# Two layers of attention and feed-forward on one core: V products issued by pairs of steps, and PSUM's working banks in two pairs

## The reference, cut to what matters

```python
x = x + _L0_xattn_ref(_layernorm(x, axis=-1), ctx_1024, L0_xattn_Wq, L0_xattn_Wk, L0_xattn_Wv, L0_xattn_Wo)
...
q = (x @ Wq).reshape(B, S, H, D).transpose(0, 2, 1, 3)
k = (c @ Wk).reshape(B, N, D, H).transpose(0, 3, 2, 1)
v = (c @ Wv).reshape(B, N, D, H).transpose(0, 3, 1, 2)
mask = jnp.all(c == 0, axis=-1)[:, None, None, :]
scores = jnp.einsum('bhsd,bhdn->bhsn', q, k) * scale
scores = jnp.where(mask, -jnp.inf, scores)
att = jax.nn.softmax(scores, axis=-1)
out = jnp.einsum('bhsn,bhnd->bhsd', att, v)
out = out.transpose(0, 2, 1, 3).reshape(B, S, H * D)
return out @ Wo
```

## Time and profile before

| | |
|---|---|
| Median of 3 runs | 2168.86 us (2168.70 to 2173.09) |
| Span of the profiled execution | 2168.4 us |
| Mean granted clock of TensorE | 0.969 of full |
| PE busy (share of the span) | 2030.2 us (94%) |
| DVE busy | 1710.2 us (79%) |
| ACT busy | 1073.8 us (50%) |
| POOL busy | 1163.8 us (54%) |
| Stages 0 to 15 of the first attention | 85 to 1616 us |
| Steady stages | 96.2 and 99.0 us in turn, 2.1 more at a turn of the loop |

### The profile page before, as it was taken

The page is one execution under the profiler, slowest core; times in us unless marked ns, Lnnn a source line. Parts: engine busy times, 40 slices in busy tenths (PEclk is TensorE's granted clock), DMA queues, the critical chain, the costliest instruction groups (busy, mean ns, idle before and its releaser), DMA issues. The chain is left out here.

```text
span 2168.4 us, 35171 instructions
## 1 busy us (share of the span) xinstructions
PE 2030.2 (94%) x10757; PEld 1431.6 (66%) x10757; DVE 1710.2 (79%) x4048; ACT 1073.8 (50%) x1493; POOL 1163.8 (54%) x624
## 2 busy tenths in 40 slices
PE   5999999999999999999999999999986899859995
PEld 4666666666666666666666666666654688647774
DVE  7788878878887888888888878878756777767764
ACT  3445445453535455454535445454533699744442
POOL 0275755657475756656575656557674354314340
PEclk9899999999999999999999999999996999979997
DMA  3000000000000000000000000000000121022210
GB/s 94 1 1 16 1 3 4 14 1 4 18 1 1 4 16 1 3 18 1 1 4 16 1 4 1 1 1 1 1 0 21 60 88 58 25 76 62 61 46 23
DMA packets 54855, 40.84 MB, mean 19 GB/s; under 512 B 2500, under 2 KB 51596, under 8 KB 53644
## 3 DMA queue, kind: packets, MB, share of 16 engines
q1 hardware_dynamic: 54668, 38.57, 6.0%
HBM read 37.45 MB, written 1.11 MB: 18 GB/s over the span
## 5 line engine op out<-in xcount | busy, mean ns | idle before, releaser
L374 POOL TENSOR_TENSOR a_den<-a_den,a_probs 128x1024 f32<-128x1024 f32 x352 | 846.7, 2408 | 362.8 <-ACT a_probs L571 362.7
L571 ACT ACTIVATE a_probs<-a_probs,a_mask_col 128x1024 f32<-128x1024 f32 x416 | 478.9, 1151 | 578.6 <-DVE a_probs L740 578.5
L740 DVE TENSOR_TENSOR a_probs<-a_scores,a_shift 128x512 f32<-128x512 f32 x832 | 566.8, 686 | 180.1 <-PE a_scores L399 162.3
L681 DVE CUSTOM_DVE_ANT_0 a_work<-a_work,a_mask_row 128x400 f32<-128x400 f32 (+1 forms) x1024 | 572.7, 587 | 35.6 <-PE a_work L431 33.2
L479 PE MATMUL a_pv<-a_probs,a_V 128*64 128x256 f32 x3328 | 451.0, 392 | 5.8 <-ACT a_outT L578 3.8
L431 PE MATMUL a_work<-a_cT_hi,a_Q_hi 128*128 128x400 f32 (+1 forms) x1024 | 357.5, 380 | 2.6
L397 PE MATMUL a_scores<-a_Q_hi,a_cT_hi 128*128 128x512 f32 x832 | 340.5, 409 | 0.1
L398 PE MATMUL a_scores<-a_Q_lo,a_cT_hi 128*128 128x512 f32 x832 | 327.9, 394 | 0.0
L399 PE MATMUL a_scores<-a_Q_hi,a_cT_lo 128*128 128x512 f32 x832 | 326.5, 392 | 0.0
L479 PEld LDWEIGHTS a_pv<-a_probs,a_V 128*64 128x64 f32 x3328 | 202.5, 136 | 186.0 <-issue 116.3
L431 PEld LDWEIGHTS a_work<-a_cT_hi,a_Q_hi 128*128 128x128 f32 x1024 | 194.9, 190 | 137.1 <-issue 89.6
(11 more groups left out here) (319 smaller groups left out, 2855.9 us busy)
## 6 DMA issues: line engine op xcount, KB each, us to landing
m_gate_rows<-gate_scratch SPq DMA_DIRECT2D x8, 1024.0 KB, 4.7
a_c_nat<-in_ctx_dram SPq DMA_DIRECT2D x8, 768.0 KB
b_c_in<-in_ctx_dram SPq DMA_DIRECT2D x8, 768.0 KB
b_c_nat<-in_ctx_dram SPq DMA_DIRECT2D x8, 768.0 KB
m_w_raw<-in_L_ffn_W_dram SPq DMA_DIRECT2D x16, 256.0 KB, 5.0
a_acc<-in_x_dram SPq DMA_DIRECT2D x8, 128.0 KB, 2.0
out_dram<-tokens SPq DMA_DIRECT2D x4, 256.0 KB, 2.3
a_V<-in_L_xattn_Wq_dram SPq DMA_DIRECT2D x1, 512.0 KB, 6.8
```

Source lines behind the costliest of these rows:

```text
L374: nc.gpsimd.tensor_tensor(half, so_far, probs[:, buffer(c, j), :], ALU.add).then_inc(den_added, 1)
L571: nc.scalar.activation(probs[:, buffer(c, j), :], probs[:, buffer(c, j), :], ACT.Exp, bias=mask_col[:, c // 2 % 2, j // 2:j // 2 + 1]).the ...
L681: nc.vector.tensor_tensor_reduce(out=X[:, bank, :w], in0=X[:, bank, :w], in1=mask_row[:, off:off + w], scale=1.0, scalar=-3e38, op0=ALU.ad ...
L740: nc.vector.tensor_tensor(probs[:, buffer(c, j), pair * 2 * S:(pair + 1) * 2 * S], Sc[:, pair, :], shift[:, first:first + 2 * S], ALU.add) ...
```

## The change

It has two parts, in the first attention alone.

1. The products with V of an even step are no longer issued in that step, but in slot 1 of the odd step after it, right before the odd step's own. An even step has none.
2. The four banks of `X` become two pairs of banks, with one semaphore pair each. An item is twice as wide and there are half as many: eight and five transposed chunks instead of four at a time, Q of four heads, V of two chunks, maxima of 804 columns (two matmuls of 402, one custom instruction on DVE, one accumulator read), a spread of 1,024 columns, one item for all eight denominators, in slot 5. An item waits until the item two before has been taken out. `V_AFTER`, `LATE_V` and `SPREAD` get new slots, so that the items keep about their places: 43 instead of 85 of them in the first 92 slots where a context is prepared, 39 instead of 77 elsewhere. The chunks hold 13 x 128 = 1,664 columns, of which the maxima now use 1,608.

The sums of all products are as before. The diff, cut to its core:

```diff
@@ -112,18 +112,19 @@
     STEPS = 2 * NC
     SLOTS = 4 * STEPS
     STAGES = 2 * B
-    PIECES = [(0, 402), (402, 400), (802, 400), (1202, 400)]
+    PIECE = 402
+    HALF = 2 * PIECE
     UNITS = G8 * 2
 
-    BANKS = 4
-    TAIL = 3
-
-    V_AFTER = [1, 4, 6, 8, 10, 12, 14, 26, 38]
-    LATE_V = [95, 97, 100, 102]
+    PAIRS = 2
+    TAIL = 2
+
+    V_AFTER = [0, 2, 4, 6, 12]
+    LATE_V = [95, 100]
     MAX_END = 92
     SHIFTS = [83, 93]
     DIAG = [84, 88]
-    SPREAD = [92, 93, 98, 99]
+    SPREAD = [92, 98]
...
-            early += [("cT", i) for i in range(3)] + [("cxT", 3)] + [("mask", i) for i in range(4)]
-        early += [("q", i) for i in range(4)]
-        vs = [("v", c) for c in range(NC)]
-        for u in range(UNITS * 4):
+            early += [("cT", 0), ("cxT", 1)] + [("mask", i) for i in range(2)]
+        early += [("q", i) for i in range(2)]
+        vs = [("v", c) for c in range(0, NC, 2)]
+        for u in range(UNITS * 2):
             early.append(("max", u))
             if u in V_AFTER:
                 early.append(vs.pop(0))
...
-            slots[3].append(("den", 0))
-            slots[7].append(("den", 1))
+            slots[5].append(("den", 0))
...
-        X = es.enter_context(nc.psum_tensor("a_work", [P, BANKS, 512], F32))
+        X = es.enter_context(nc.psum_tensor("a_work", [P, PAIRS, 2, 512], F32))
...
-                            filled(pool, it, use_of(the_plan(it, c), "den", j - 2))
+                            filled(pool, it, use_of(the_plan(it, c), "den", 0))
...
-                    for ch in range(4 * i, min(4 * i + 4, NC)):
-                        last = nc.tensor.transpose(out[:, ch % 4 * P:(ch % 4 + 1) * P], c_nat[:, ch, :], ident[:, :])
+                    for ch in range(8 * i, min(8 * i + 8, NC)):
+                        last = nc.tensor.transpose(out[:, ch % 8 * P:(ch % 8 + 1) * P], c_nat[:, ch, :], ident[:, :])
                     if kind == "cxT":
                         pe.wait_ge(xn_ready, at(it, 2, s // 2 + 1))
                         for j in range(2):
-                            last = nc.tensor.transpose(out[:, (j + 1) * P:(j + 2) * P], xn_b[:, j, :], ident[:, :])
+                            last = nc.tensor.transpose(out[:, (j + 5) * P:(j + 6) * P], xn_b[:, j, :], ident[:, :])
                 elif kind == "mask":
-                    pe.wait_ge(flag_done, at(it, 8, s // 2 * 4 + i + 1))
-                    off, w = PIECES[i]
-                    last = nc.tensor.matmul(out[:, :w], ones_b[:, :], c_flag[:, off:off + w], start=True, stop=True)
+                    pe.wait_ge(flag_done, at(it, 4, s // 2 * 2 + i + 1))
+                    for k in range(2):
+                        off = (2 * i + k) * PIECE
+                        last = nc.tensor.matmul(X[:, bank, k, :PIECE], ones_b[:, :], c_flag[:, off:off + PIECE],
+                                                start=True, stop=True)
                 elif kind == "q":
-                    for k in range(2):
-                        h = s % 2 * G8 + 2 * i + k
+                    for k in range(4):
+                        h = s % 2 * G8 + 4 * i + k
                         last = split_product(out[:, k * S:(k + 1) * S], [g[:, h, :] for g in G], xnT,
                                              slice(0, D), slice(0, S))
                 elif kind == "v":
-                    last = split_product(out, cT[s // 2 % 2], Wv, slice(i * P, (i + 1) * P),
-                                         slice(s % 2 * G8 * HD, (s % 2 + 1) * G8 * HD))
+                    for k in range(min(2, NC - i)):
+                        last = split_product(X[:, bank, k, :], cT[s // 2 % 2], Wv, slice((i + k) * P, (i + k + 1) * P),
+                                             slice(s % 2 * G8 * HD, (s % 2 + 1) * G8 * HD))
                 elif kind == "max":
-                    off, w = PIECES[i % 4]
-                    last = nc.tensor.matmul(out[:, :w], Q[s % 2][0][:, i // 4 * P:(i // 4 + 1) * P],
-                                            cT[s // 2 % 2][0][:, off:off + w], start=True, stop=True)
+                    for k in range(2):
+                        off = (i % 2 * 2 + k) * PIECE
+                        last = nc.tensor.matmul(X[:, bank, k, :PIECE], Q[s % 2][0][:, i // 2 * P:(i // 2 + 1) * P],
+                                                cT[s // 2 % 2][0][:, off:off + PIECE], start=True, stop=True)
                 elif kind == "spread":
-                    if i < 2:
-                        pe.wait_ge(diag_done, at(it, 32, 8 * s + 4 * (i + 1)))
-                    else:
-                        pe.wait_ge(shift_steps, at(it, 20, 5 * s + 5))
-                    last = nc.tensor.matmul(out, ones_r[:, :], shift_diag[:, i % 2 * 4:i % 2 * 4 + 4, :], start=True, stop=True)
+                    for k in range(2):
+                        if i == 0:
+                            pe.wait_ge(diag_done, at(it, 32, 8 * s + 4 * (k + 1)))
+                        elif k == 0:
+                            pe.wait_ge(shift_steps, at(it, 20, 5 * s + 5))
+                        last = nc.tensor.matmul(X[:, bank, k, :], ones_r[:, :], shift_diag[:, 4 * k:4 * k + 4, :],
+                                                start=True, stop=True)
                 elif kind == "den":
 
-                    pe.wait_ge(den_added, at(it, 4 * (STEPS - 2), c * (STEPS - 2) - 1 + i))
-                    for k in range(2):
+                    for k in range(4):
+                        if k % 2 == 0:
+                            pe.wait_ge(den_added, at(it, 4 * (STEPS - 2), c * (STEPS - 2) - 1 + k // 2))
                         for odd in range(2):
-                            h = 4 * i + 2 * k + odd
+                            h = 2 * k + odd
                             last = nc.tensor.matmul(out[HD * odd:HD * odd + HD, k * S:(k + 1) * S], ones[:, :],
                                                     den[:, h * S:(h + 1) * S], start=True, stop=True)
...
-                        if part == 1:
-
-                            pv(it, c, j, 0)
-                            pv(it, c, j, 1)
+                        if part == 1 and j % 2 == 1:
+
+                            for both in (j - 1, j):
+                                pv(it, c, both, 0)
+                                pv(it, c, both, 1)
                         elif part > 1 and j + 2 < STEPS:
...
-                    nc.scalar.activation(V[:, s % 2, i, :], X[:, bank, :], ACT.Copy).then_inc(bank_free[bank], 1)
+                    n = min(2, NC - i)
+                    nc.scalar.activation(V[:, s % 2, i:i + n, :], X[:, bank, 0:n, :], ACT.Copy)\
+                      .then_inc(bank_free[bank], 1)
                 elif kind == "spread":
                     if c >= 0:
 
-                        act.wait_ge(shifted, shifts_of(it, c, STEPS - 2 + i // 2, i % 2 + 1))
-                    nc.scalar.activation(shift[:, i * 512:(i + 1) * 512], X[:, bank, :], ACT.Copy)\
+                        act.wait_ge(shifted, shifts_of(it, c, STEPS - 2 + i, 2))
+                    nc.scalar.activation(shift[:, i * 1024:(i + 1) * 1024], psum, ACT.Copy)\
                       .then_inc(bank_free[bank], 1)
                 elif kind == "den":
-                    nc.scalar.activation(rden[:, i * 512:(i + 1) * 512], X[:, bank, :], ACT.Copy)\
-                      .then_inc(bank_free[bank], 1)
+                    nc.scalar.activation(rden[:, :], psum, ACT.Copy).then_inc(bank_free[bank], 1)
...
-                    off, w = PIECES[i % 4]
                     filled(dve, it, use)
                     dve.nop(nofuse=True)
-                    nc.vector.tensor_tensor_reduce(out=X[:, bank, :w], in0=X[:, bank, :w],
-                                                   in1=mask_row[:, off:off + w], scale=1.0, scalar=-3e38,
+                    masks = mask_row[:, i % 2 * HALF:(i % 2 + 1) * HALF].rearrange("p (h n) -> p h n", h=2)
+                    nc.vector.tensor_tensor_reduce(out=X[:, bank, :, :PIECE], in0=X[:, bank, :, :PIECE],
+                                                   in1=masks, scale=1.0, scalar=-3e38,
                                                    op0=ALU.add, op1=ALU.max, accum_out=maxes[:, s % 2, i:i + 1])\
                       .then_inc(bank_free[bank], 1)
                 elif kind == "shift":
                     half = UNITS // 2
                     units = slice(i * half, (i + 1) * half)
...
-                        for quarter in (2 * j, 2 * j + 1):
-                            taken(dve, it, prep_use(it, c - 1, "spread", quarter))
+                        taken(dve, it, prep_use(it, c - 1, "spread", j))
```

More of the change, by code:

```diff
@@ L149, in prep_slots @@
             slots[DIAG[i]].append(("diag", i))
-        for i in range(4):
+        for i in range(2):
             slots[SPREAD[i]].append(("spread", i))
@@ L248, in attention_0 @@
         xn_all, wv_ready = sem("xn_all"), sem("wv_ready")
-        bank_full = [sem(f"bank{i}_full") for i in range(BANKS)]
```

(12 more changed lines are left out.)

74 lines of the change are left out of this document (36 added, 38 removed).

## The result

The changed kernel takes 2189.7 us (median; 2188.3 to 2191.9), 1.0084 of the kernel before, 95% interval [1.0070, 1.0097]: **slower by 0.84%** (the kernel before ran in 2170.9 us beside it), where 2162 was forecast. Its profiled execution spans 2188.9 us, 20.5 more than before. By the traces of the two, 11.0 of these lie in the opening stage (the first score product starts at 91.76 instead of 80.80), 8.5 between it and the last addition to the tokens (1560.96 instead of 1552.45), and 1 in the rest of the program.

The account below looks back on a forecast made before the run. PE sets the time in the first attention, with DVE close behind. Mode changes saved -78, waits +73, opening -2.5, a denominator copy +1: -6.5 us, from 2168.86 to 2162 us; this case 2148 to 2177, overall range 2110 to 2200.

Parts of the forecast that it names:

- The detour: PE's mode change between 64- and 128-column matmuls in the first attention: 0.35 us each, fifteen saved a stage, -78 us.
- 2x + y: PE, V and denominator products back to back: two groups of eight V matmuls (x) plus one mode change (y), 2.08 us.
- The pair of maxima: DVE, one maximum over two banks: 0.95 us start to start, 1.06 if nothing of two instructions is saved.
- rival (c): DVE, steps 9 to 22: pair of maxima costs 1.06 us, +32, 2194 us; chance 0.26 including unsaved mode changes.
- The waits for single late operands: PE waits: context stage 1.2 us for xn_b, 0.9 at mask product, 0.6 at first maxima; spread 1.25 in each stage.
- The waits in steps 3 to 22: PE waits: steps 3 to 7, 1.75 us context stage, 0.7 head stage; steps full of maxima, 1.25 and 1.0.
- The opening stage: Before the loop, bound by DVE: 3.5 us saved on maxima, 1 lost to coarser Q and spread, -2.5 us.
- The last stage, GpSimd, and ScalarE's fewer copies: Last stage 0, GpSimd's first two sums nothing, ScalarE's fewer copies nothing apart from the walked waits.
- coarser hand-over: Banks handed over in halves, even steps without V products: PE waits 7.0 us a context stage, 3.05 a head stage, +73.
- rival (a): Stages of the first attention: waits are half of those walked, 36 us lost instead of 73, 2125 us; chance 0.25.
- The rule weighed: Skill's rule on unsaturated engines causing bubbles: break instructions up; by it the change, which enlarges them, would be slower.

Follow-up runs that it names:

- the extra matmuls: Changed kernel with one more 512-column matmul behind each of the 32 pairs of maxima in the opening stage: 2183.3 us, 1.0067.
- the control: Kernel before with the same 32 extra 512-column matmuls in its opening stage, one behind every second maximum: 2167.0 us, 0.9989.

## Why the prediction was wrong

Forecast by the spans 2161.9, measured 2188.9: 27 us, 13.5 in the opening stage, 12.5 from its end to the last addition, 1 in the rest.

- **The detour: right.** From the first of two 402-column matmuls over 16 V matmuls to the next pair's first are 2.44 us; two lone groups are 2 x 1.22 by the earlier trace rows, and this one, less 0.36 for the two of 402, is 2.08, the prediction's 2x + y. 0.36 is saved.
- **The pair of maxima: right, a little cheap even.** 0.91 us (810.44 to 811.35), not 0.95; rival (c) did not happen, though its premise, that DVE's price reaches PE, holds. The prediction said that no row spoke for less than 0.95; the first two maxima of the earlier trace rows start 0.49 apart, and by its own sum that gives 0.91.
- **The waits for single late operands: right** in place and size. Walked 1.2, 0.9, 0.6 and 1.25; measured 1.1 (xn_b), 0.9 (flags), 0.7 (first maxima) and 1.1 us (spread, in each stage). In a context and a head stage 4.8 us against 5.2.
- **The waits in steps 3 to 22: too small, a step that failed.** The two stages save 15 x 0.36 x 2 = 10.8 us of detours and are 1.1 longer, so they wait 11.9, where 10.05 was walked. Less the named ones that is 7.1 against 4.85: 2.25 more in two stages, offset by 0.4 of named waits and 0.3 of detours; 7.5 times the remaining 1.6 is the 12. (The stage behind the loop turn adds its 2.7, and the first and the last stages give about as much back.) It is many small gaps: from start to next start, the score matmuls of a context stage took 37.0 us before and take 40.3. The walk took "first and last around the even step's scores" as free and looked for PE's wait at the maxima. The run with couples of maxima shows what it left out: two maxima in one slot hold up the scores' subtraction, and PE's next score product waits for that (16.0 us in 39 waits instead of 3.9 in 14).
- **The opening stage: the step that failed outright.** -2.5 was said and +11.0 came. The working counted what DVE saves and took DVE as the bound, since the earlier trace rows has PE waiting for it. It did not walk the round of one buffer. In the second half that is 0.2 us hand-over, 1.04 for two matmuls at the half clock, 0.15, and 0.92 on DVE, 2.3, which two buffers don't hide: the 3.5 us were not saved. In the first half a V item keeps one of the two for its six matmuls and its copy, and this, with the wider mask and Q products ahead, is 10.6 of the 11 us. That the hand-over does it, and not the order, is shown by the run with that order and four banks (first score product at 79.96); that the half clock has a share of 5.4 us, by the extra matmuls. With four single banks DVE is busy with the three others for 3 x 0.53 = 1.6 us while PE fills one with one matmul, and the control shows that this is enough. The prediction reads the granted clock for the stages only; for this stretch the same view gives 0.51.
- **The last stage, GpSimd, and ScalarE's fewer copies: right**, at nothing. The last stage's V groups stand 5.23 us apart, as two steps of 2.61 before.
- **What the prediction called the added thing.** It put every wait under "coarser hand-over". In the stages the halves cost 8 us net (of the wide instructions' gain) and the order that came with them 41; in the opening the halves cost 12. The two were never separated, so the forecast could not say that the gain was to be had: with four banks and the order of before, 2124.5 and 2126.4 us ran. That rival (a) has 2125 is chance, since it spoke of the changed kernel.
- **The rule weighed** (the Trainium skill, "Perfetto Trace Analysis", "Optimizing Scalar/DVE Operations": break instructions up where an unsaturated engine causes bubbles). The runs agree in part only: all items broken up, each half handed over by itself, gain 18 us in the same order (2171.6 for 2189.7), most of it in the opening; maxima broken up with the pair still handed over as one cost 17 us more; and two narrow maxima in one slot cost 39 us over the same two in neighbouring slots. The place of an instruction in the queue decided more here than its size.

Open is why the parts of the order don't add in the way they do. For the small gaps between matmuls in the full steps PE's waits name no single releaser.

The version to take is the one with four banks, paired V products, denominators in slot 5, and V items in couples or not: 2123.0 and 2124.5 us, 0.9787 of the kernel before both, 3% faster than the changed kernel.

## What to carry to other kernels

Take a change apart into what an instruction does, how many buffers are handed over, and where the items stand in an in-order queue, and price each; here the useful part (fewer mode changes, -43 us) hid behind the third. Work of one engine that used to cover another's latency (V products in every step) is worth its place: after gathering it, spread the other work evenly over the steps that lost it. For every ring of buffers, add up one round (hand-over, fill at the clock that is granted then, hand-over, drain) and divide by the number of buffers, even where one engine looks like the clear bound.

## What the runs showed of the hardware

- A change between matmuls on 64 and on 128 columns costs PE 0.36 us, and a group of 16 in one mode pays it once. The Trainium skill, "TensorEngine Tiling (Array Packing)", section "Key Properties", says that switching the tiling mode drains the engine. The drain as such stands in no view; a cost at each change of mode agrees with it, and the rows give it this length, there and back.
- A DVE reduction over two PSUM banks (804 elements) takes 0.91 us from start to next start in the stages and 0.96 in the opening with extra matmuls, one over a single bank 0.49 or 0.53.
- With one matmul more behind each pair the granted clock from 70 to 80 us was 1.00 (2.4 GHz) instead of 0.50 and 0.51, in both kernels, and only the one with two buffers gained by it.
- A wait of PE can cost more than its length. Behind waits of 4.16 us for Q's operand the granted clock was 0.50 for 3.4 to 10.2 us each time, seven times in seven; behind a wait of 2.24 us for xn_b at a loop turn of the changed kernel it was so for 6.6, and behind the same wait at the next turn (2.29 us) not at all. The kernel before, and the one with V products paired alone, have no such stretch in their stages.
